# Gating at the expert's eviction and an adding scatter in a macaron block with routed experts, on one core

## What is computed

```python
def _L0_ffn_ref(x, router_w, router_bias, sw1, sw3, sw2, ew1, ew2):
    shared_out = jax.nn.silu(xf @ sw1) * (xf @ sw3) @ sw2
    s = jax.nn.sigmoid(xf @ router_w.T)
    _, topk_idx = jax.lax.top_k(s + router_bias, 2)            # 2 of 8 experts
    gates = s_sel / (s_sel.sum(axis=1, keepdims=True) + 1e-09)
    h = jax.nn.gelu(jnp.einsum('nd,edh->neh', xf, ew1), approximate=False)
    y = jnp.einsum('neh,ehd->ned', h, ew2)
    return shared_out + jnp.einsum('ned,ne->nd', y, comb)      # comb: the two gates
...
x = x + 0.5 * _L0_ffn_ref(_layernorm(x), ...)
x = x + _L0_attn_ref(_layernorm(x), Wq, Wk, Wv)   # rfft of q, k, v; cumsum(fk * fv); irfft
x = x + 0.5 * _L0_ffn_ref(_layernorm(x), ...)
```

## Time and profile before

| what | value |
| --- | --- |
| three timed runs | 2063.09, 2069.51, 2073.0 us; median 2069.51 |
| span of the profiled execution | 2101.2 us |
| PE, DVE busy | 1652.2 us (79%), 1419.4 us (68%) |
| ACT, POOL busy | 656.2 us (31%), 767.4 us (37%) |
| bytes read from and written to DRAM | 91.03 MB, 81.89 MB |

### The profile page before, as it was taken

The page is one execution under the profiler, slowest core; times in us unless marked ns, Lnnn a source line. Parts: engine busy times, 40 slices in busy tenths (PEclk is TensorE's granted clock), DMA queues, the critical chain, the costliest instruction groups (busy, mean ns, idle before and its releaser), DMA issues.

```text
span 2101.2 us, 35984 instructions
## 1 busy us (share of the span) xinstructions
PE 1652.2 (79%) x10302; PEld 1458.4 (69%) x10303; DVE 1419.4 (68%) x3362; ACT 656.2 (31%) x1094; POOL 767.4 (37%) x868
## 2 busy tenths in 40 slices
PE   3999999679999647676767775599999967999940
PEld 2788888669999536555555553478888857999940
DVE  4778787535555368979898987377877753555557
ACT  3333333134444223232322231233333313444410
POOL 0454443324444323333333332144444422444420
PEclk9999999889999867776777776599999978999975
DMA  8211111144444311010101000011111114444459
GB/s 275 76 52 41 51 51 44 44 122 131 134 134 129 102 41 41 20 40 20 40 20 40 20 20 0 31 55 50 44 54 47 45 46 122 133 132 136 129 183 349
DMA packets 123782, 170.37 MB, mean 81 GB/s; under 512 B 14881, under 2 KB 105394, under 8 KB 123442
## 3 DMA queue, kind: packets, MB, share of 16 engines
q1 hardware_dynamic: 89938, 91.05, 15.0%
q0 software_dynamic: 25344, 70.29, 9.1%
q10 hardware_dynamic: 8448, 8.39, 1.1%
HBM read 91.03 MB, written 81.89 MB: 82 GB/s over the span
## 4 chain that ended last, share of the span: by engine, by line
PE 58%; DVE 17%; issue 9%; DMA 7%; ACT 3%; POOL 3%; SPq 2%; another core or an unknown queue 0%; DVEq 0%; POOLq 0%; ACTq 0%
PE bank L608 17%; PE bank L610 16%; PE bank L609 15%; PE bank L723 3%; DMA lists<-a_rows,a_slots 3%; POOL lists L405 3%; PE bank L733 2%; DMA f_yf<-results 2%; DVE t_cum L1151 2%; DVE t_rn L1133 2%; DVE a_gate_u L971 1%; PE bank L827 1%; DVE X L1214 1%; PE bank L632 1%; DVE t_pr L1149 1%
## 5 line engine op out<-in xcount | busy, mean ns | idle before, releaser
L416 POOL DMA_INDIRECT results<-b_yb,b_goal x272 | 261.6, 962 | 370.5 <-DVE b_yb L1074 297.8
L405 POOL DMA_INDIRECT lists<-a_rows,a_slots x256 | 259.7, 1014 | 117.5 <-issue 64.5
L1074 DVE COPY b_yb<-bank 128x512 f32<-128x512 f32 x136 | 94.1, 692 | 188.4 <-PE bank L610 180.0
L608 PE MATMUL bank<-t_xah,t_wfh 128*128 128x512 f32 x192 | 114.0, 594 | 111.8 <-DVE t_xal L848 61.7
L608 PE MATMUL bank<-ew_h,b_hth 128*128 x544 | 161.5, 297 | 20.3 <-issue 9.9
L608 PE MATMUL bank<-ew_h,b_xbth 128*128 x544 | 165.3, 304 | 1.0 <-DVE b_xbtl L848 1.0
L608 PE MATMUL bank<-a_sw2h,a_uh 128*128 128x256 f32 x512 | 150.4, 294 | 12.6 <-DVE a_ul L848 7.3
L455 ACT ACTIVATE b_hth<-bank 128x512 fp32r<-128x512 f32 x136 | 81.3, 598 | 246.7 <-PE bank L723 239.5
L609 PE MATMUL bank<-ew_l,b_xbth 128*128 x544 | 152.8, 281 | 0.0
L610 PE MATMUL bank<-ew_h,b_xbtl 128*128 x544 | 152.4, 280 | 0.0
L610 PE MATMUL bank<-ew_h,b_htl 128*128 x544 | 152.3, 280 | 0.0
(11 more groups left out here) (209 smaller groups left out, 5114.0 us busy)
## 6 DMA issues: line engine op xcount, KB each, us to landing
b_xb<-lists SPq DMA_DIRECT2D x272, 132.0 KB
t_yg<-results SPq DMA_DIRECT2D x32, 512.0 KB, 4.7
f_yf<-results SPq DMA_DIRECT2D x32, 512.0 KB, 10.9
X<-in_L_attn_x SPq DMA_DIRECT2D x16, 512.0 KB
out<-X ACTq DMA_DIRECT2D x16, 512.0 KB, 7.1
results<-b_yb,b_goal POOLq DMA_INDIRECT x272
w_raw_ew<-in_L_ffn_ew SPq DMA_DIRECT2D x2, 2048.0 KB, 14.3
lists<-a_rows,a_slots POOLq DMA_INDIRECT x256
```

The lines of the kernel that those rows point to most:

```text
L405: pool.indirect_dma_start(out=lists, out_offset=bass.IndirectOffsetOnAxis(ap=slots[:, q, k, j:j + 1], axis=0), in_=rows[:, q, j, :], in_of ...
L416: pool.indirect_dma_start(out=results, out_offset=bass.IndirectOffsetOnAxis(ap=goal[:, slot, blk:blk + 1], axis=0), in_=YB[:, slot, blk, : ...
L608: pe.matmul(o, a("h"), b("h"), start=first, stop=False)
L1074: dve.tensor_copy(YB[:, slot].rearrange("p b d -> p (b d)"), bank[:, 7 - par, :]).then_inc(s_yok, 1)
```

## The change

The gates are written to two spare columns of `rows`, travel with the row through the list, and are applied when an expert's result leaves PSUM: two instructions of 128x256 with a scalar for each partition stand in place of one copy of 128x512. Since the gate must be in the row before it is scattered, `gate` moves ahead of `places`, and POOL waits for both and then scatters all eight. There is a list for each expert and choice (16, `LISTS`), 70 pairs instead of 68, first all of choice 0, then all of choice 1; between the two halves POOL waits until every scatter has landed. The result is not scattered to a place of its own but added in DRAM to `sums`, which SP has filled with `X` (with the shared output in it) chunk by chunk during phase A. The attention phase loads `X` from there; at the end the output is copied from DRAM to DRAM. `sums` and `lists` get filler rows by DMA at the program's start. A slot of `XB` holds the gate until the result has left PSUM, so it is loaded again only then.

```diff
-BLOCKS = TOPK * TILES + E
+LISTS = TOPK * E
+RB = TILES + E - 2
+BLOCKS = TOPK * RB
...
+SPARE = E * P
+RS = E * CAP + SPARE
+TRASH = LISTS * P + TOPK * SPARE
...
-            sp.dma_start(lists[E * CAP:E * CAP + E * P, :], fill[E * P:2 * E * P, :]).then_inc(s_spare, 16)
+            for r in range(TOPK):
+                sp.dma_start(lists[r * RS + E * CAP:(r + 1) * RS, :],
+                             c_fill[LISTS * P + r * SPARE:LISTS * P + (r + 1) * SPARE, :]).then_inc(s_spare, 16)
+            for i in range(2):
+                sp.dma_start(sums[i][TOKENS:TOKENS + TRASH, :], c_fill[:, 0:D]).then_inc(s_spare, 16)
...
+            def store_base(layer):
+                def step(c, par, half):
+                    sp.wait_ge(s_xout, c * 2 + (2 * CH * layer + 2))
+                    sp.dma_start(sums_d[layer][:, bass.ds(c * J, J), :],
+                                 X[:, bass.ds(c * J, J), :]).then_inc(s_base, 16)
...
                 def step(n, slot, q):
-                    atleast(sp, s_bl, n + (p0 - 3) if not isinstance(n, int) or n >= 4 else 0)
+                    atleast(sp, s_yok, n + (p0 - 3) if not isinstance(n, int) or n >= 4 else 0)
...
-            sp.wait_ge(s_mlo, 3)
-            def load_results(c, par, half):
-                atleast(sp, s_comb, c)
-                for k in range(2):
-                    sp.dma_start(YG[:, k, :, :], res_d[:, k, bass.ds(c * J, J), :]).then_inc(s_yg, 16)
...
+            for i in range(8):
+                sp.dma_start(out_d[:, i * 8:(i + 1) * 8, :], sums_d[1][:, i * 8:(i + 1) * 8, :]).then_inc(s_store, 16)
...
                         pool.indirect_dma_start(
-                            out=results,
+                            out=sums[layer],
                             out_offset=bass.IndirectOffsetOnAxis(ap=goal[:, slot, blk:blk + 1], axis=0),
-                            in_=YB[:, slot, blk, :], in_offset=None).then_inc(s_ysc[slot], 16)
-                run_steps(pool, step, 0, 4, PAIRS, PAIRS, 4)
+                            in_=YB[:, slot, blk, :], in_offset=None, compute_op=ALU.add).then_inc(s_ysc[slot], 16)
+                pool.wait_ge(s_base, 16 * CH * (layer + 1))
+                run_steps(pool, step, 0, 0, HALF - 3, HALF, 4)
+                for i in range(4):
+                    pool.wait_ge(s_ysc[i], YW[i] * layer + 32 * ((HALF - i + 3) // 4))
+                run_steps(pool, step, HALF, HALF + 1, PAIRS - 2, PAIRS, 4)
...
                     if nxt:
                         hidden(s + 1, 0)
+                        gate(s + 1, 1 - par)
                         places(s + 1, 1 - par)
                         hidden(s + 1, 1)
                     if far:
                         dve.wait_ge(s_xh, s + (g0 + 3))
                         low(XT["l"][:, par], bank[:, 0:2, :], XT["h"][:, par]).then_inc(s_xl, 1)
-                    if nxt:
-                        gate(s + 1)
...
-                        dve.tensor_copy(YB[:, slot].rearrange("p b d -> p (b d)"), bank[:, 7 - par, :]).then_inc(s_yok, 1)
+                        for blk in range(2):
+                            ins = dve.tensor_scalar(YB[:, slot, blk, :], bank[:, 7 - par, blk * D:(blk + 1) * D],
+                                                    XB[:, slot, blk, D + 1 + r:D + 2 + r], None, ALU.mult)
+                        ins.then_inc(s_yok, 1)
```

More of the change, by code:

```diff
@@ L109, in run_steps @@
     n0 = tally.n if tally else 0
+    if b == a:
+        for s in range(b, hi):
+            step(s, s % unroll, s // unroll)
+        return
     with eng.Fori(0, (b - a) // unroll) as i:
@@ L208, in build @@
         goal = place("b", "goal", [P, 4, 2], I32)
-        over = place("b", "over", [1, E, TILES], F32)
+        over = place("b", "over", [1, LISTS, TILES], F32)
         past = place("b", "past", [1, 2, BLOCKS, E], F32)
@@ L284, in build @@
         out_d = out.rearrange("b s d -> (b s) d").rearrange("(t p) d -> p t d", p=P)
-        res_d = results[0:2 * TOKENS, :].rearrange("(k t p) d -> p k t d", p=P, k=2)
-        YW = PAIRS // 4 * 32
+        sums_d = [a[0:TOKENS, :].rearrange("(t p) d -> p t d", p=P) for a in sums]
+        YW = [32 * n for n in TURNS]
         block = ctx.enter_context(nc.Block())
@@ L317, in _ @@
             run_steps(sp, load_x, 0, 2, CH, CH, 2)
+            def store_base(layer):
[3 more added lines that the diff above has]
+                                 X[:, bass.ds(c * J, J), :]).then_inc(s_base, 16)
+                run_steps(sp, step, 0, 2, CH, CH, 2)
             def phase_b(layer):
                 sp.wait_ge(s_table, layer + 1)
[L321 to L326 removed]
+                for i in range(LISTS):
+                    end = sp.value_load(table[0:1, 2 * BLOCKS + i:2 * BLOCKS + i + 1], min_val=0,
+                                        max_val=(TOPK - 1) * RS + (E - 1) * CAP + TOKENS)
+                    sp.dma_start(lists[bass.ds(end, P), :], c_fill[i * P:(i + 1) * P, :]).then_inc(s_tail, 16)
+                sp.wait_ge(s_tail, LISTS * 16 * (layer + 1))
+                sp.wait_ge(s_spare, 64)
                 sp.wait_ge(s_scat, 2 * J * 16 * CH * (layer + 1))
@@ L943, in gate @@
-                    ins.then_inc(s_gated, 1)
+                    dve.tensor_tensor(rows[:, par, :, D + 1:D + 1 + TOPK].rearrange("p j k -> p k j"), both,
+                                      bc(gsum[:, 20:24].unsqueeze(1), [P, TOPK, J]), ALU.add).then_inc(s_gated, 1)
                 def places(c, par):
                     g = c + g0
-                    ch.link(dve.scalar_tensor_tensor(pick2[:, 0], cnt, 1.0, msk, ALU.is_equal, ALU.mult))
-                    ch.settle()
-                    ch.link(dve.tensor_tensor(pick2[:, 1], msk, pick2[:, 0], ALU.subtract))
@@ L1034, in block_table @@
                 ch.settle()
-                ch.link(dve.tensor_tensor_scan(cb, cst[one, C_ONE8:C_ONE8 + E], nb, 0.0, ALU.mult, ALU.add))
+                ch.link(dve.tensor_tensor_scan(cb, cst[one, C_RESE:C_RESE + LISTS], nb, 0.0, ALU.mult, ALU.add))
                 ch.settle()
                 blk = cst[one, C_BLK:C_BLK + BLOCKS]
-                ch.link(dve.tensor_tensor(past[:, 0], bc(blk.unsqueeze(2), [1, BLOCKS, E]),
-                                          bc(cb.unsqueeze(1), [1, BLOCKS, E]), ALU.is_ge))
+                for r in range(TOPK):
+                    its, ends = slice(r * RB, (r + 1) * RB), cb[:, r * E:(r + 1) * E]
+                    ch.link(dve.tensor_tensor(past[:, 0, its], bc(blk[:, its].unsqueeze(2), [1, RB, E]),
+                                              bc(ends.unsqueeze(1), [1, RB, E]), ALU.is_ge))
                 ch.settle()
-                ch.link(dve.tensor_tensor(past[:, 1], past[:, 0], bc(nb.unsqueeze(1), [1, BLOCKS, E]), ALU.mult))
+                for r in range(TOPK):
+                    its, sizes = slice(r * RB, (r + 1) * RB), nb[:, r * E:(r + 1) * E]
+                    ch.link(dve.tensor_tensor(past[:, 1, its], past[:, 0, its], bc(sizes.unsqueeze(1), [1, RB, E]),
+                                              ALU.mult))
                 ch.settle()
@@ L1047, in block_table @@
                 ch.settle()
-                ch.link(dve.tensor_scalar(line[:, 5], line[:, 5], float(P), None, ALU.mult))
+                for r in range(TOPK):
+                    its = slice(r * RB, (r + 1) * RB)
+                    ch.link(dve.tensor_scalar(line[:, 5, its], line[:, 5, its], float(P), float(r * RS), ALU.mult, ALU.add))
                 ch.settle()
@@ L1054, in phase_b, with step @@
                 p0 = PAIRS * layer
-                def step(s, u, q):
+                def step(s, u, q, r):
                     par = u % 2
```

207 lines of the change are left out of this document (81 added, 126 removed).

## The result

The changed kernel is slower by a factor of 1.1075 (95% interval 1.1041 to 1.111). It took 2287.33 and 2293.09 us, against a median of 2067.66 us. The forecast was 2200 us with a range of 2125 to 2290: the direction is right, and the time, 2290.2 between the two runs, lies on the upper end of the range. The sum said +132 us; the change cost some 222.

What follows compares the result with a forecast made beforehand. Bounds: PE in phase A (DVE at `a_xtl`), mostly PE in phase B, DVE busiest in attention, DMA at the end. Terms summed to +132 us on a 2101.2 span, 2233, scaled to 2200 us; range 2125 to 2290.

Steps and rivals of the forecast that it cites:

- the rival on the slow add: Phase B: a slow adding scatter sets the pace; an add 5 us longer gives +84, 2283; chance 0.19.
- the loop of the destinations: Phase B: eviction, POOL's scatter issues, landing, `b_goal`, products, next eviction; put at 4P = 10.1 + x + P.
- the slot's loop: Phase B: eviction of n - 4, loads, transposes and eviction of n in four periods; P 4.55, taken as 4.4.
- Start, +27: Program start: 9.47 MB of filler ahead of x on SP's queue delays the first statistics, +27 us (25 to 51).
- The low end: Start: filler moves at 371 GB/s, 25.5 us, rather than 51 if copying from DRAM to DRAM costs both directions.
- Phase A, +62: Phase A: `gate` before `places` (+1.9) and longer `route` (+0.6) delay `a_xtl`; 2.2 us a chunk, +62 (0 to 75).
- Fillers and table, +22.6: Between phases A and B: 16 lists' filler issues (+10.1) and table instructions (+1.2), twice, nothing hiding them: +22.6 us.
- Phase B, the slot, +53: Phase B: XB's slot reloaded only after eviction raises the period from 3.99 to 4.4 us a pair, +53 (20 to 75).
- Phase B, the add, "hidden": Phase B: the add may take 3 us longer before costing anything; taken as hidden, +3 for draining.
- The sign that was named for a slow add: Phase B: `b_goal` as the releaser would show the forecast wrong and the add slow.
- Attention, -7: Attention: line 1087's work saves 0 in the loop, in the shadow of line 1103's wait; entry -9.6, x load +3.
- End, -46: End: the 73.2 us become an 8.39 MB copy of 25 us plus 2.4 for landing, -46 (-26 to -48).

Runs made afterwards that it cites:

- e5: The kernel before, unchanged, run and profiled again beside the changed one: 2061.35 us.
- e6: The changed kernel, unchanged, run once more beside the kernel before: 2288.79 us, ratio 1.109.
- e4: The changed kernel with the fillers of lists and sums behind the 16 loads of x on SP's queue: 2318.42 us, ratio 1.1099.
- e12: The changed kernel without `gate`'s ten DVE instructions, one memset in their place: 2246.75 and 2233.78 us.
- e7: The changed kernel with `gate` behind `a_xtl` again and POOL waiting for it before scattering: 2283.78 us, ratio 1.1073.
- e1: The changed kernel with token and gate columns copied to a small tile, so XB's slot is free again at `b_xbtl`: ratio 1.0676.
- e9: The kernel before with one edit, SP loading an XB slot only after the result of four pairs before left PSUM: 2169.39 us, ratio 1.0331.
- e2: The changed kernel with a scatter that overwrites instead of adding: ratio 1.0852.
- e3: The changed kernel with token and gate columns copied out of XB, and `b_goal` with its scatter wait moved to just before the eviction: ratio 1.0331.

## Why the prediction was right, and where its sizes were off

The direction and the loop that sets the pace were forecast; that the time still lies within the range owes something to luck. By e5 and e6 the sum is 95 us short: phase B alone is short by 108, and phase A gives 24 back. The upper end of the range stands where it does for the rival on the slow add, which put the extra time into the loop of the destinations; the time got there mostly by the slot's loop.

- **Start, +27.** Right in mechanism and size (+28.8). DMA moved 326 GB/s from 16 to 50 us, against the 371 reckoned with; x did not overtake the filler, and e4 gets it 30 us sooner. The low end was the one to take. The rule of the Trainium skill that the forecast named (DMA: Bandwidth & Descriptors, Queues, rings and completion order) agrees with these runs.
- **Phase A, +62.** `gate` ahead of `a_xtl` was the right cause, shown by e12; measured +37.6 on the chip of e5 and e6. The mis-sized terms: `gate` and `places` cost +1.4 us on DVE where +1.9 stood (ten instructions of `gate` take 1.85), and the +0.6 for the longer `route` (3.48 us in place of 2.76) does not reach the time: e12 has that route and a phase A as short as before. Where it is taken up is seen only in part: DVE's wait for `a_uh` behind it falls from 1.26 us to 1.00, the means of ten chunks of e5 and e6. That `gate` would be free behind `a_xtl` was right only for the old order; e7 shows what it costs in the new one.
- **Fillers and table, +22.6.** Measured +23.3.
- **Phase B, the slot, +53.** The right loop, e1 and e9 show it, but two sizes were off. The sum itself gave 4.55, of which I took 4.4; e9 measured 4.53 for that loop alone. The 4.3 us from eviction to transposes are 4.16 in e9 and 4.27 in e2, so the term was right for a plain scatter; beside the adding one it is 4.99, since the loads land later, which the forecast priced at nothing. The base was off as well: 3.99 us a pair of the earlier trace rows is not PE's own pace, which is 3.8. Together 1.2 us a pair in place of 0.4.
- **Phase B, the add, "hidden".** Wrong. The step that failed is the sum of the rival on the slow add, 4P = 10.1 + x + P, which lets the add be 3 us slow for nothing. It missed who is queued behind `b_goal`: the eviction of n + 2. The loop closes over two periods and not over four; e1 shows it, at 4.37 against 3.82 in e3, and e2 shows that even behind the other loop the add costs 0.32 us a pair. It takes 0.6 us more of POOL for each issue; I had looked only at its landing. The sign that was named for a slow add, `b_goal` as a releaser, did show in the changed kernel; e1 and e9 settle that the slot's loop came first.
- **Attention, -7.** Measured -3.8, and the period of the attention loop did not change (+0.1 us from the first to the last `t_rn` of e5 and e6): the 54 us of line 1087 lay in the shadow of line 1103's waits, as forecast. Those waits in e5 and e6 (now line 1104):

```profile
DVE X L1103 <- PE bank L828: 34.5, 22, 5.7
```

```profile
DVE X L1104 <- PE bank L835: 86.7, 30, 5.6
```

- **End, -46.** Measured -39.9. Eight copies of 1.05 MB moved at 308 GB/s, and 6.8 us passed between the last eviction and the first copy, for the last adding scatters.

The Trainium skill (Collectives: The Full Stack, The bandwidth ceiling) says of collectives that an add needs two source reads for each chunk, and that ReduceScatter, which adds, so runs at half the rate of AllGather, which copies. Here the share of DMA in the first phase B is 0.36 in e2 and 0.65 in the changed kernel, with the add; in e3, with the same scatters in less time, it is 0.85. The runs agree in direction with a higher cost of these scatters. DMA's share did not reach 1; the price in time came from the issue and from the loads beside it.

## What to carry to other kernels

When a value is now kept longer in a buffer, write down the whole loop of that buffer (release, issue, landing, use, next release) and compare its length with the period, even where the wait looks harmless: four slots gave two periods of slack here, and the loop needed 10.3 us. Copying the few bytes that are needed late into a place of their own (one DVE instruction a pair) opened it, and a wait that stands early in an engine's order for something used late belongs where it is used. And whatever must be known before a transfer starts moves with it everything that waits for that transfer to land: ask for that before you move it on one engine.

## What the runs showed of the hardware

- An indirect DMA of 128 rows of 1 KB with an add takes 1.56 us of POOL to issue, the same one without 0.96 (the changed kernel and e2 above). Target and indices are the same in both.
- One unchanged program ran phase B at 3.99 us a pair in one execution and at 3.79 in another, at nearly the same granted clock (0.99 and 1.00); the kernel before took 2061 to 2101 us on different chips, so only kernels run side by side were compared by time.
- 9.47 MB more of filler from DRAM to DRAM, most of it in rows of 1 KB, delayed the first statistics by 28.8 us (e6 against e5), 329 GB/s. Loads and the old filler moved 371 GB/s; the feared doubling of cost didn't come.
